# Scattered rows carry the token's score as extra columns, the score goes into the routed Silu and product, and the scatter has three row buffers

## The reference

```
x = x + cross_attention_0(layernorm(x), ctx)
x = x + shared_ffn(layernorm(x)) + routed_ffn(layernorm(x))
x = x + cross_attention_1(layernorm(x), ctx, ctx)
x = x + tree_ffn(layernorm(x))
```

```
logits = x @ gate_w
score = sigmoid(max(logits));  expert = argmax(logits)
xs = x * score
routed = (silu(xs @ rt_gate[expert]) * (xs @ rt_up[expert])) @ rt_down[expert]
```

## Time and profile before

| | |
|---|---|
| three timed runs | 892.91, 897.83, 898.03 us; median 897.83 us |
| the profiled execution: span from its first to its last instruction | 890.3 us (its own time isn't given beside it) |
| TensorE matmul busy | 821.5 us, 92% |
| VectorE busy | 650.6 us, 73% |
| ScalarE busy | 545.3 us, 61% |
| GpSimd busy | 250.1 us, 28% |
| mean granted TensorE clock | 0.985 of full speed |

### The profile page before, as it was taken

The page is one execution under the profiler, slowest core; times in us unless marked ns, Lnnn a source line. Parts: engine busy times, 40 slices in busy tenths (PEclk is TensorE's granted clock), DMA queues, the critical chain, the costliest instruction groups (busy, mean ns, idle before and its releaser), DMA issues.

```text
span 890.3 us, 15056 instructions
## 1 busy us (share of the span) xinstructions
PE 821.5 (92%) x4236; PEld 618.0 (69%) x4277; DVE 650.6 (73%) x1695; ACT 545.3 (61%) x947; POOL 250.1 (28%) x328
## 2 busy tenths in 40 slices
PE   4899998887589969999999999999999999999997
PEld 2677776666556746667777777777777777777775
DVE  3677778876574326587788888878887888788774
ACT  2365566555333313536777777787877687777765
POOL 1112112177717725012033213321321232131000
PEclk9899999999799989999999999999999999999999
DMA  5236575453235424210000000000000000000000
GB/s 143 58 93 166 157 212 154 126 143 112 81 93 154 133 74 121 71 47 22 4 25 24 18 6 24 24 7 17 24 24 0 24 24 24 0 24 13 13 1 24
DMA packets 91421, 55.66 MB, mean 63 GB/s; under 512 B 13439, under 2 KB 88183, under 8 KB 91255
## 3 DMA queue, kind: packets, MB, share of 16 engines
q1 hardware_dynamic: 74304, 40.38, 16.1%
q0 software_dynamic: 4096, 8.40, 3.3%
q10 hardware_dynamic: 12983, 6.41, 2.5%
HBM read 32.10 MB, written 23.07 MB: 62 GB/s over the span
## 4 chain that ended last, share of the span: by engine, by line
PE 62%; POOL 10%; DVE 9%; issue 7%; ACT 6%; DMA 3%; ACTq 1%; another core or an unknown queue 1%; DVEq 0%; POOLq 0%; SPq 0%
PE PS L742 7%; PE PS L987 7%; PE PS L1009 6%; PE PS L1011 6%; PE PS L1010 6%; PE PS L988 6%; PE PS L989 6%; POOL x_sorted L497 5%; PE PS L998 4%; PE PS L760 3%; POOL rs L482 2%; PE PS L996 2%; PE PS L923 2%; POOL xs L490 2%; DVE xn L1069 2%
## 5 line engine op out<-in xcount | busy, mean ns | idle before, releaser
L697 ACT ACTIVATE sil<-PS,b_in_c 128x512 f32<-128x512 f32 x256 | 161.9, 684 | 112.4 <-PE PS L996 68.1
L1374 DVE TENSOR_TENSOR sil_l<-sil,sil_h 128x512 fp32r<-128x512 f32 x256 | 164.7, 684 | 44.9 <-ACT sil_h L705 44.2
L480 POOL TENSOR_TENSOR ve<-mv,eps 128x4 f32<-128x4 f32 x64 | 17.3, 271 | 504.8 <-DVE mv L1063 504.7
L705 ACT ACTIVATE sil_h<-sil 128x512 fp32r<-128x512 f32 x224 | 128.9, 631 | 0.0
L1009 PE MATMUL PS<-sil_h,wout_l 128*128 128x512 f32 x256 | 121.4, 474 | 1.7 <-DVE sil_l L1374 1.7
L1358 DVE TENSOR_SCALAR dec<-PS,b_in_c 128x512 bf16<-128x512 f32 x128 | 95.4, 745 | 25.3 <-PE PS L989 25.3
L987 PE MATMUL PS<-x4T_h,win_l 128*128 128x512 f32 x256 | 102.5, 400 | 0.9 <-ACT sil L697 0.4
L1011 PE MATMUL PS<-sil_h,wout_h 128*128 128x512 f32 x256 | 100.6, 393 | 0.0
L1010 PE MATMUL PS<-sil_l,wout_h 128*128 128x512 f32 x256 | 100.5, 393 | 0.0
L988 PE MATMUL PS<-x4T_l,win_h 128*128 128x512 f32 x256 | 99.8, 390 | 0.0
L989 PE MATMUL PS<-x4T_h,win_h 128*128 128x512 f32 x256 | 99.8, 390 | 0.0
(11 more groups left out here) (146 smaller groups left out, 1615.8 us busy)
## 6 DMA issues: line engine op xcount, KB each, us to landing
x_sorted<-zeros SPq DMA_DIRECT2D x4, 1280.0 KB, 7.2
xs_in<-x_sorted SPq DMA_DIRECT2D x20, 256.0 KB, 3.0
y_sorted<-yo ACTq DMA_DIRECT2D x20, 256.0 KB, 2.3
X<-in_x SPq DMA_DIRECT2D x16, 256.0 KB, 6.5
rows<-xn SPq DMA_DIRECT2D x16, 256.0 KB, 2.5
xs<-rows SPq DMA_DIRECT2D x16, 256.0 KB, 3.2
out<-res SPq DMA_DIRECT2D x16, 256.0 KB, 2.4
ctxT<-in_ctx_t SPq DMA_DIRECT2D x16, 240.0 KB, 5.1
```

The lines of the kernel that those rows point to most:

```text
L697: act.activation(tile(sil[p % 2], c, W), bank(2 * (p % 2) + c), ACT.Silu, bias=b_in_c[:, 2 * p + c:2 * p + c + 1]).then_inc(t_silu, 1)
L705: act.activation(tile(sil_h[p % 2], c, W), tile(sil[p % 2], c, W), ACT.Copy).then_inc(t_hi, 1)
L1374: dve.tensor_tensor(tile(sil_l[p % 2], c, W), tile(sil[p % 2], c, W), tile(sil_h[p % 2], c, W).bitcast(F32), ALU.subtract).then_inc(t_lo, 1)
```

## The change

A row in `x_sorted`, `xs` and `xs_in` gets four more columns (RW = 132 instead of 128 floats, 528 bytes). GpSimd no longer multiplies the rows with the score. It writes the score into the four extra columns (`write_scores`), for the next group before it scatters the present one, and the scatter takes its indices straight from `POS`. There are three buffers `xs` instead of two, in the part of the arena that the trees' weights fill later; `load_rows` is issued for other groups at each place (three at once at the start of each half), and the loops of half 1 on GpSimd and SyncE are written out. In the routed stage VectorE copies the four scores of a unit from `xs_in` to `scr` (`r_scores`), ScalarE's Silu takes a tile's score as its scale, and VectorE multiplies the up product with the score and the Silu. Both are then one instruction of 128x256 per tile instead of one of 128x512 for two tiles. SyncE's load of a unit also waits for the copy of the scores (`r_sc`). TensorE's turn reads at a step of 132.

```diff
+RW = P + 4
+XW = G * RW
+XB = 3
...
-    x_sorted = [nc.dram_tensor(f"x_sorted{h}", (HTILES * P, P), F32, kind="Internal").ap() for h in range(HALVES)]
+    x_sorted = [nc.dram_tensor(f"x_sorted{h}", (HTILES * P, RW), F32, kind="Internal").ap() for h in range(HALVES)]
...
+        xs = [cut.take(f"xs{i}", XW) for i in range(XB)]
...
-            def load_rows(k, v, i):
-                if not below(i, 1):
+            def load_rows(k):
+                v, i = k % XB, k // XB
+                if i:
                     sp.wait_ge(scattered[v], 16 * G * i)
                 sp.wait_ge(a_rows, 16 * (k + 1))
-                sp.dma_start(by_tile(xs[v]), rows2[bass.ds(k * G, G), :, :].rearrange("b s d -> s b d")
+                sp.dma_start(by_tile(xs[v], RW)[:, :, 0:P], rows2[k * G:(k + 1) * G, :, :].rearrange("b s d -> s b d")
                              ).then_inc(k_in[v], 16)
...
                 if g == HG:
-                    load_rows(0, 0, 0)
-                    load_rows(1, 1, 0)
+                    for k in range(XB):
+                        load_rows(k)
                 if g > HG + 4:
-                    i = g - HG - 4
-                    load_rows(2 * i, 0, i)
-                    load_rows(2 * i + 1, 1, i)
+                    for k in range(2 * (g - HG - 4) + 1, min(2 * (g - HG - 4) + 3, HG)):
+                        load_rows(k)
                 load_later(g)
                 a_body(g, g % 2, g < NG - 2)
...
-                sp.dma_start(by_tile(xs_in[u]),
+                sp.dma_start(by_tile(xs_in[u], RW),
                              slots(x_sorted, r, h)).then_inc(r_in[u], 16)
             def r_next(r, u, h):
                 sp.wait_ge(r_xT_ps, r + 1)
+                sp.wait_ge(r_sc, r + 1)
                 r_load(r + 2, u, h)
-            for u in range(2):
-                sp.wait_ge(scattered[u], 16 * G * (HG // 2))
+            def all_scattered(units):
+                for v in range(XB):
+                    sp.wait_ge(scattered[v], 16 * G * len(range(v, units, XB)))
+            all_scattered(HG)
             sp.wait_ge(a_pv_ps, NG)
             r_load(0, 0, 0)
             r_load(1, 1, 0)
-            load_rows(HG, 0, HG // 2)
-            load_rows(HG + 1, 1, HG // 2)
-            for u in range(2):
-                r_next(u, u, 0)
-            with sp.Fori(0, HR // 2 - 2) as i:
-                for u in range(2):
-                    r_next(2 * i + 2 + u, u, 0)
-                    load_rows(HG + 2 + 2 * i + u, u, HG // 2 + 1 + i)
-            for u in range(2):
-                sp.wait_ge(scattered[u], 16 * G * (NG // 2))
+            for k in range(HG, HG + XB):
+                load_rows(k)
+            for r in range(HR - 2):
+                r_next(r, r % 2, 0)
+                if r > 1 and HG + XB + r - 2 < NG:
+                    load_rows(HG + XB + r - 2)
+            all_scattered(NG)
...
-            def scale_rows(k, v, i):
+            def write_scores(k):
+                v, i = k % XB, k // XB
+                if i:
+                    pool.wait_ge(scattered[v], 16 * G * i)
+                pool.tensor_copy(by_tile(xs[v], RW)[:, :, P:],
+                                 SCORE[:, k * G:(k + 1) * G].unsqueeze(2).to_broadcast([P, G, RW - P])).then_inc(k_score, 1)
+            def scatter(k, h):
+                v, i = k % XB, k // XB
                 pool.wait_ge(k_in[v], 16 * (i + 1))
-                pool.tensor_copy(idx[:, v, :], cols(POS, k * G, G))
-                pool.tensor_copy(sco[:, v, :], cols(SCORE, k * G, G)).then_inc(k_idx, 1)
-                pool.wait_ge(k_idx, k + 1)
-                pool.tensor_tensor(by_tile(xs[v]), by_tile(xs[v]),
-                                   sco[:, v, :].unsqueeze(2).to_broadcast([P, G, P]), ALU.mult).then_inc(k_scaled, 1)
-            def scatter(k, v, h):
-                pool.wait_ge(k_scaled, k + 1)
+                pool.wait_ge(k_score, k + 1)
                 pool.sem_inc(pool_passed, 1)
                 for j in range(G):
-                    pool.indirect_dma_start(x_sorted[h], bass.IndirectOffsetOnAxis(ap=idx[:, v, j:j + 1], axis=0),
-                                            tile(xs[v], j), None).then_inc(scattered[v], 16)
+                    at = k * G + j
+                    pool.indirect_dma_start(x_sorted[h], bass.IndirectOffsetOnAxis(ap=POS[:, at:at + 1], axis=0),
+                                            tile(xs[v], j, RW), None).then_inc(scattered[v], 16)
             def a_body(f, g, l, m, u, units=(), route=None):
...
                         pool.wait_ge(scored, 1)
-                    scale_rows(units[0], 0, units[0] // 2)
-                    scatter(units[0], 0, 0)
-                    scale_rows(units[1], 1, units[0] // 2)
+                        write_scores(0)
+                    write_scores(units[1])
+                    scatter(units[0], 0)
                 if g is not None:
                     rstd(1, g, a_mv2, a_ve2, a_rs2)
                 if units:
-                    scatter(units[1], 1, 0)
+                    if units[1] + 1 < HG:
+                        write_scores(units[1] + 1)
+                    scatter(units[1], 0)
             phase_a(a_body, pool)
             pool.wait_ge(placed, 2)
             pool.wait_ge(scored, 2)
-            with pool.Fori(0, HG // 2) as i:
-                for v in range(2):
-                    k = 2 * i + HG + v
-                    scale_rows(k, v, HG // 2 + i)
-                    scatter(k, v, 1)
+            write_scores(HG)
+            for k in range(HG, NG):
+                if k + 1 < NG:
+                    write_scores(k + 1)
+                scatter(k, 1)
...
-            def r_silu(q, v):
+            def r_silu(q, v, u):
                 act.wait_ge(r_gu_ps, q + 1)
-                pair = by_tile(PS[:, 512 * (1 + 2 * v):512 * (3 + 2 * v)], 512)
-                act.activation(by_tile(sg[v], FI), pair[:, :, 0:FI], ACT.Silu).then_inc(r_sg, 1)
+                for t in range(2):
+                    i = act.activation(tile(sg[v], t, FI), bank(1 + 2 * v + t, FI), ACT.Silu,
+                                       scale=scr[:, u, 2 * v + t:2 * v + t + 1])
+                i.then_inc(r_sg, 1)
...
             def r_body(r, u, stores):
-                r_silu(2 * r, 0)
+                act.wait_ge(r_sc, r + 1)
+                r_silu(2 * r, 0, u)
                 if not last_unit(r):
                     r_evac_x(r + 1, 1 - u)
-                r_silu(2 * r + 1, 1)
+                r_silu(2 * r + 1, 1, u)
...
             def r_turn(r, u):
                 pe.wait_ge(r_in[u], 16 * (r // 2 + 1))
-                turn(bank(0), xs_in[u], P, P, r_xT_ps)
+                for j in range(G):
+                    i = pe.transpose(tile(bank(0), j), xs_in[u][:, j * RW:j * RW + P], IDENT)
+                i.then_inc(r_xT_ps, 1)
...
-            def r_mul(q, v):
+            def r_scores(r, u):
+                dve.wait_ge(r_in[u], 16 * (r // 2 + 1))
+                dve.tensor_copy(scr[:, u, :], by_tile(xs_in[u], RW)[:, :, P]).then_inc(r_sc, 1)
+            def r_mul(q, v, u):
                 dve.wait_ge(r_sg, q + 1)
                 if not below(q, 2):
                     dve.wait_ge(r_aT_ps, q - 1)
-                pair = by_tile(PS[:, 512 * (1 + 2 * v):512 * (3 + 2 * v)], 512)
-                dve.tensor_tensor(by_tile(ract[v], FI), by_tile(sg[v], FI), pair[:, :, FI:], ALU.mult).then_inc(r_act, 1)
+                for t in range(2):
+                    i = dve.scalar_tensor_tensor(out=tile(ract[v], t, FI), in0=bank(1 + 2 * v + t)[:, FI:],
+                                                 scalar=scr[:, u, 2 * v + t:2 * v + t + 1], in1=tile(sg[v], t, FI),
+                                                 op0=ALU.mult, op1=ALU.mult)
+                i.then_inc(r_act, 1)
...
-            def r_half(q, v):
-                r_mul(q + 1, 1 - v)
-                r_evac_a(q, v)
+            def r_first_half(r, u):
+                r_scores(r + 1, 1 - u)
+                r_mul(2 * r + 1, 1, u)
+                r_evac_a(2 * r, 0)
+            def r_second_half(r, u):
+                r_mul(2 * r + 2, 0, 1 - u)
+                r_evac_a(2 * r + 1, 1)
+            r_scores(0, 0)
             a_first_slots(1)
-            r_mul(0, 0)
-            r_half(0, 0)
+            r_mul(0, 0, 0)
+            r_first_half(0, 0)
             a_slots(1)
-            r_half(1, 1)
+            r_second_half(0, 0)
             a_pack(1)
-            with dve.Fori(1, HR + 1) as r:
-                r_half(2 * r, 0)
```

31 lines of the change are left out of this document (18 added, 13 removed).

## The result

The changed kernel took 906.66 us (median of 4 runs, 905.10 to 908.40), the kernel before in the same series 897.53 us (892.91 to 898.03): a ratio of 1.0122, with a 95% interval of 1.0094 to 1.0151. The forecast was 885.7 us in a range of 877 to 895. The kernel became slower where it was forecast faster.

A forecast was written before the change was run, and what follows sets the result against it. The prediction saw mostly TensorE bounding the kernel, with about a tenth GpSimd, so only GpSimd's scattering in phase A's end and the routed stage could give time. 7.3 + 9.6 - 4.8 = 12.1 us off 897.83 gave 885.7, range 877 to 895.

The forecast's parts named there:

- Term 1: End of phase A: without GpSimd's product, rounds shrink from 16.24 to 14.5 us and the last to 12.9; 7.3 us gained.
- Term 2: Routed stage: faster scatter groups of half 1 remove TensorE's wait at unit 10 and the slow unit behind; 9.6 us gained.
- Term 3: Routed stage: Silu and product, each split in two with a scalar per partition, lengthen the units' chain; 4.8 us lost.
- (c): Rival: scatters get dearer with 528-byte rows, kernel slower from 0.36 us more each, 906.9 us at 0.5; chance of over 897: 0.10.
- (a): Rival: the split of Silu and product is free, 16.9 us gained, 880.9 us; chance 0.14 for this and below, to 877.
- (b): Rival: the split of Silu and product is dear, only 3.4 us gained, 894.4 us; chance 0.18 together with (d).
- (d): Rival: only phase A or the wait at unit 10 gives time, 895.3 or 893.0 us; chance 0.18 together with (b).

The follow-up runs named there:

- full series: Series whose traces hold 8,102 to 8,154 semaphore-count records; in one, the unaltered changed kernel, run again, took 883.58 us, ratio 0.9882 to the kernel before.
- e7_phase_a: Kernel before, with GpSimd's product of rows and scores left out in the first half alone: 889.59 us, ratio 0.9924.
- e4_split: Kernel before, with Silu and its product each issued as two 128x256 instructions, the second with constant 1 as scalar: 895.36 us, ratio 0.9998.
- thin: Series whose traces hold 6,128 to 6,378 semaphore-count records; in one, the unaltered changed kernel, run a third time, took 904.00 us, ratio 1.0087.
- e5_nowait: Changed kernel plus an unused 1.03 us GpSimd product between the second half's scatter groups, its end not waited for: 884.80 us, ratio 0.9866; again 888.82 us, 0.9919.

## Why the prediction was wrong

**Term 1, -7.3 us: right, but for a late count.** Rounds of 14.67 us where 14.5 were forecast (16.24 before). The last round took 13.02 us in the full series (forecast 12.9) and 15.92 us in the first result: 2.9 us more, of which the late counts in VectorE's rows above are 2.3. Between the same two `rs` as above lie 58.24 us before, 51.31 in the full series (6.9 less), 51.45 in `e7_phase_a` and 54.76 in the first result (3.5 less). The start of the turn of unit 0 alone is a poor measure: with one and the same phase A it lies anywhere from 243.3 to 251.8 us in eleven traces. VectorE's `xn` of the first norm stayed at 1.30 us where 1.1 was forecast (1.89 before), since the last of its four instructions took 0.53 us instead of 0.35. It isn't the scatter beside it: in `e7_phase_a` an `xn` beside a scatter took 1.13 us. The new copy of the scores on GpSimd stands just ahead of the slow ones and is missing in `e7_phase_a`; no run parts its cost.

**Term 2, -9.6 us: this is the step that failed.** In the full series each of its own numbers came out: groups of 5.14 us (forecast 5.3 to 5.4), the last scatter at 296.57, no wait at unit 10 (304.84 and 311.67 us are the turns of units 9 and 10), no slow unit behind it. In the first result only the first groups came so fast (5.15 us); the later ones took 12.1, 9.0, 7.5 and 6.4 us, the last scatter started at 318.54 us, where before it started at 317.96, and unit 10 (336.58, 6.9 us after unit 9) found its rows there only because the hole had made it late as well. The step counted what a shorter group does for the last row and said that the row loads behind the turns don't bind; it took for granted that TensorE's units go on at their pace beside denser scatters. In the first result the units 3 to 4 took 17.5 us longer than one should, more than the whole sum. The row loads did then bind, as its consequence: the count that SyncE waited for was late, so GpSimd stood 7.13 us for rows, up to 291.80.

**Term 3, +4.8 us: about right in size, with the weight on the wrong part.** Units of 6.7 us against 6.53 us (forecast 6.68). By the turns, unit 0 to 9 took 1.9 us and unit 11 to 19 1.7 us longer in the full series than before, 3.6 us for 17 of the 19 steps and so some 4 us in all; the waits for `actT` are in this (four, 3.6 us in all, where the earlier trace rows had 2.1). The pairs took 0.83 and 0.88 us (forecast 0.8 and 0.87). The step counted two instructions and the operand together; `e4_split` (0.9998, 0.9973 to 1.0022) shows that the splitting costs nothing that can be measured, and the operand from a tile is what costs.

**The sum** of -12.1 us holds where the counts aren't late: 896.40 - 883.58 = 12.8 us less. In spans, full is 11.6 us under before (878.7 and 890.3), and the first result 26.1 us over full: 17.5 us at unit 3, 2.9 us in phase A's last round, 4.5 us of first loads and clock, which is no work of the change, 1.0 us at the late turn of unit 13, and 0.2 us left over.

**The rivals.** (c) had the right time, 906.9 us, for a wrong reason: scatters of 528-byte rows took GpSimd 977 ns each where those of before took 986 ns. The trouble was not the price of a scatter, but that scatters came closer together. (a), (b) and (d) have nothing in them that could hold a count. None of my rivals asked what TensorE's neighbours see of it when another engine's gaps close. What the prediction drew from the Trainium skill against the change (page DMA: Bandwidth & Descriptors, section How a descriptor splits into AXI transactions: up to 1.1 us more for the load of `xs_in`) doesn't show here: in the full series the median load of 264 KB took 2.9 us, before 3.0 us for 256 KB.

**Could it have been foreseen?** Not from the one trace of before: it is of the full kind, and all its turns are seen after 0.04 us. What the trace did show was that the product left a pause of 2.2 us in every group; that it was of use to another engine it did not.

**What stays open.** What makes a series thin, and whether the counts are held by the same thing that loses their records. The page NOTIFIC — the notification-queue block of the Trainium skill (section 7.1 Overflow: three behaviours, one of which stalls the engine) says that a full ring of trace records either drops new ones, overwrites old ones or holds back the engine that produces them. Missing records and held counts do go together here, in all seven thin traces with scatters under 1.5 us apart. Against a simple tie stands that records are missing from 404 us on too, where no time is lost, and that only TensorE's counts are late. No run here was made without recording, so none shows whether the hole would be there without it: that the recording makes the late counts is a rival that nothing here excludes. Also open is why it is TensorE's counts alone: in the same stretch VectorE's product started 0.03 us after ScalarE's Silu, at 272.31, and TensorE 0.14 us after VectorE's copy, at 275.20.

**The better version** is `e5_nowait`: 0.9866 of before in a full series (the changed kernel 0.9882, no difference that can be told) and 0.9919 in a thin one, where the changed kernel is at 1.0087. It beats the kernel before in both.

## What to carry to other kernels

Before an instruction is taken off an engine that only seems to cost time, ask what its time was between: here 1 us of useless work per four scatters was worth 15 us in one condition of the chip and nothing in another. When a wait's releaser reads "remote" and two engines start in the same instant long after the producer's row has ended, compare the end of the producer with the start of the waiting one, and ask whether the work was late or only its count. And one series on one chip was not enough to judge this change: the same program was 1.2% slower and 1.2% faster than the kernel before, each time with an interval of less than 0.6% to either side.

## What the runs showed of the hardware

- TensorE's semaphore counts can be seen up to 15.6 us after the instruction's end, while GpSimd issues indirect scatters of 128 rows one in 1.28 us; at one in 1.6 us the delay was between 0.04 us, as without scatters, and 0.8 us. Only in series whose traces lack a fifth to a quarter of the counts' records; 0.04 us at 1.28 us in the other. ScalarE's, VectorE's and GpSimd's counts were not late in either (0.03 us at most where they can be matched).
- Gathers do it too: one in 1.26 us, and a turn was seen 1.0 us late in the thin series.
- Scalar operands from a tile cost: ScalarE's 128x256 Silu 471 ns against 383 ns with a constant, VectorE's 128x256 two-operation product 477 against 417 ns.
- Two halves of 128x256 took 0.66 us on ScalarE and 0.76 us on VectorE, one of 128x512 took 0.59 and 0.69 us: splitting cost nothing that could be measured (0.9998 of before), in a chain that had 0.3 us of slack.
- A scatter of 128 rows takes GpSimd 0.97 to 0.99 us on the mean and 0.30 us to the next, with 512 or 528 bytes a row.
